# A two-layer kernel on eight cores: another order for the first eight tiles

## What is computed

```python
x = L0_attn_x
xn = layernorm(x)                                  # no scale, no shift
z, h = sigmoid(xn @ Wz.T + bz), xn @ Wh.T + bh
s = affine_scan(log(1 - z + 1e-8), z * h)          # along T
g = silu((silu(xn @ Wg.T) * (xn @ Wu.T)) @ Wd.T)   # int weights / 127
x = x + s * g
xn = layernorm(x)
q, k, v = split(xn @ W_qkv.T)
s = softmax(q @ k.T / 32) @ v
r, kk = sigmoid(mix_r(xn) @ W_r.T), mix_k(xn) @ W_k.T
g = silu(r * (relu(kk) ** 2 @ W_v.T))
x = x + s * g
```

## Time and profile before

| | us |
|---|---|
| three runs: median, lowest, highest | 1232.82, 1171.05, 1410.46 |
| the profiled execution | 1171.72 |
| its span on the slowest core (core 0) | 1170.6 |
| spans of all cores | 1168.2 to 1170.6 |
| PE busy on core 0 | 1145.4 (98%) |
| PE busy in 10 to 15, 15 to 20 and 20 to 25 us of core 0 | 3.57, 2.94, 4.13 |

### The profile page before, as it was taken

How to read it: one execution, slowest core, us unless ns; L and a number is a source line. 1 busy time by engine, 2 the same in 40 slices (tenths; PEclk the granted TensorE clock), 3 DMA queues, 4 the chain that set the end, 5 groups by cost and what they waited for, 6 DMA issues and landing times.

```text
span 1170.6 us, 15141 instructions; the slowest of 8 cores (1168.2 to 1170.6 us)
## 1 busy us (share of the span) xinstructions
PE 1145.4 (98%) x5315; PEld 527.5 (45%) x5422; DVE 550.2 (47%) x700; ACT 251.6 (21%) x317; POOL 137.6 (12%) x257
## 2 busy tenths in 40 slices
PE   5999999999999999999999999999999999999998
PEld 3444444444444444444444444444444444444444
DVE  4333331555657663225557884011134445555565
ACT  4211111122123111112212723533110110110110
POOL 3222221110111111101011122220000000000000
PEclk8999999999999999999999999999999999999999
DMA  9996678545554765545543579994000105255665
GB/s 212 211 143 103 91 121 185 108 108 103 119 103 72 168 122 81 80 81 107 107 102 61 84 127 156 150 157 112 1 19 18 37 18 121 71 124 115 138 137 160
DMA packets 96522, 126.91 MB, mean 108 GB/s; under 512 B 48192, under 2 KB 52544, under 8 KB 96448
## 3 DMA queue, kind: packets, MB, share of 16 engines
q0 software_dynamic: 31104, 65.03, 35.7%
q1 hardware_dynamic: 65344, 60.91, 19.8%
HBM read 159.47 MB, written 20.97 MB: 154 GB/s over the span
## 4 chain that ended last, share of the span: by engine, by line
PE 97%; DVE 1%; DMA 1%; issue 1%; ACT 0%; SPq 0%; POOL 0%; DVEq 0%; ACTq 0%; POOLq 0%
PE PS L156 96%; DMA S<-xtok 1%; DVE S L160 0%; PE PS L293 0%; SPq L127 0%; DVE S L284 0%; DVE S L911 0%; DVE S L306 0%; DVE BN L243 0%; ACT S L281 0%; DVE BN L244 0%; ACT S L309 0%; PE PS L880 0%; PE PS L879 0%; POOL MV L264 0%
## 5 line engine op out<-in xcount | busy, mean ns | idle before, releaser
L156 PE MATMUL PS<-S 128*128 128x512 bf16 x5157 | 1131.7, 379 | 7.4 <-ACT S L771 0.9
L156 PEld LDWEIGHTS PS<-S 128*128 128x128 bf16 x5264 | 514.6, 98 | 616.3 <-issue 4.8
L160 DVE TENSOR_TENSOR S<-S,PS 128x512 bf16<-128x512 bf16 x96 | 66.0, 688 | 182.9 <-PE PS L156 169.8
L404 ACT ACTIVATE S<-PS 128x512 bf16<-128x512 f32 x96 | 57.3, 597 | 258.5 <-PE PS L156 199.2
L851 ACT ACTIVATE S<-PS,CB 128x2048 bf16<-128x2048 f32 x16 | 31.5, 1967 | 225.0 <-DVE CB L849 209.4
L160 DVE TENSOR_TENSOR S<-S 128x512 f32<-128x512 f32 (+2 forms) x60 | 62.9, 1048 | 6.5 <-DVE S L569 0.3
L847 DVE TENSOR_REDUCE CB<-PS 128x1 f32<-128x1024 f32 x32 | 39.2, 1225 | 54.9 <-PE PS L880 33.1
L748 DVE SCALAR_TENSOR_TENSOR S<-S,PS 128x1024 f32<-128x1024 f32 x16 | 19.5, 1222 | 83.8 <-PE PS L156 83.5
L469 ACT ACTIVATE S<-PS 128x512 bf16<-128x512 f32 x32 | 19.1, 597 | 172.9 <-PE PS L156 172.9
L127 POOL DMA_DIRECT2D S<-wg x48 | 28.4, 592 | 232.6 <-PE PS L156 230.9
L798 DVE CAST S<-PS 128x512 bf16<-128x512 f32 x32 | 22.1, 692 | 48.3 <-PE PS L156 46.8
(11 more groups left out here) (77 smaller groups left out, 401.7 us busy)
## 6 DMA issues: line engine op xcount, KB each, us to landing
S<-wg POOLq DMA_DIRECT2D x48, 256.0 KB, 4.7
S<-wu POOLq DMA_DIRECT2D x48, 256.0 KB, 5.7
S<-wd POOLq DMA_DIRECT2D x16, 768.0 KB, 7.5
S<-xtok SPq DMA_DIRECT2D x16, 512.0 KB, 9.6
S<-xt SPq DMA_DIRECT2D x16, 512.0 KB, 16.2
x1s<-S SPq DMA_DIRECT2D x16, 512.0 KB, 2.6
S<-x1s SPq DMA_DIRECT2D x32, 256.0 KB, 4.4
out<-S SPq DMA_DIRECT2D x31, 256.0 KB, 3.1
```

Of the source, the lines that this page charges most:

```text
L156: ins = te.matmul(dst, l, r, start=(i == 0), stop=(i == n - 1))
L160: return DVE.did(ve.tensor_mul(o, a, b))
L404: at = ACT.did(se.activation(sil, ps(bg), AF.Silu, scale=1.0 / 127.0))
```

## The change

- Tile 1 and tile 3 are asked for by ScalarE's queue, tile 0, the identity and tile 2 by SyncE's. Tiles 4 and 5 are asked for by SyncE behind a wait for tile 1's statistics, tiles 6 and 7 and the two small matrices behind a wait for tile 3's.
- The first weight pair is asked for behind tile 1's root and bias, no longer behind tile 0's; the second pair behind tile 3's root, the third behind tile 4's, the fourth, as before, behind tile 5's.
- Tile 2's statistics and norm go to VectorE; `ln0_stats_act` is gone, and each root is for one tile. Tiles 0, 1 and 2 are copied from PSUM by ScalarE right behind their transposes, tile 3 by VectorE.
- `keep_warm` is called with 24, 8, 8 and 12 instead of 24, 4 and 10, one call behind each of the four transposes.

```diff
-        def xk_load(i):
-            xk_tok.append(dma(SYN, x_tile(i), xk[i * 128:(i + 1) * 128, :], xk_sem[i % 8]))
+        def xk_load(i, line=SYN):
+            xk_tok.append(dma(line, x_tile(i), xk[i * 128:(i + 1) * 128, :], xk_sem[i % 8]))
 
         xk_load(0)
         i_tok = dma(SYN, ident[:], identd, i_sem)
-        for i in range(1, 8):
-            xk_load(i)
-        c_tok = dma(SYN, CB[:, 0:32], cb, c_sem)
-        c_tok = dma(SYN, ones[:], onesd, c_sem)
+        xk_load(1, ACT)
+        xk_load(2)
+        xk_load(3, ACT)
...
         ln0_stats(0)
         ln0_rstd(0)
         ln0_bias(0)
-        POOL.after(xk_tok[1])
-        w_pair()
-        w_pair()
         ln0_norm(0, True)
-        ln0_transpose(0, True, False)
+        ln0_transpose(0)
         keep_warm(24)
         ln0_stats(1)
+        SYN.after(ln0_tok[1])
+        xk_load(4)
+        xk_load(5)
         ln0_rstd(1)
         ln0_bias(1)
-        ln0_stats_act(2)
+        w_pair()
         ln0_norm(1, True)
-        ln0_transpose(1, True, False)
-        keep_warm(4)
+        ln0_transpose(1)
+        keep_warm(8)
+        ln0_stats(2)
+        ln0_rstd(2)
         ln0_stats(3)
-        ln0_copy(0, True)
-        ln0_rstd(2, 2)
-        ln0_bias(2, True)
+        SYN.after(ln0_tok[3])
+        xk_load(6)
+        xk_load(7)
+        c_tok = dma(SYN, CB[:, 0:32], cb, c_sem)
+        c_tok = dma(SYN, ones[:], onesd, c_sem)
+        ln0_rstd(3)
         w_pair()
-        ln0_norm(2, True)
+        ln0_norm(2)
+        ln0_transpose(2)
+        keep_warm(8)
         ln0_norm(3)
-        ln0_transpose(3, True, False)
-        ln0_copy(1, True)
-        ln0_copy(3, True)
-        ln0_transpose(2)
-        keep_warm(10)
+        ln0_transpose(3, True)
+        keep_warm(12)
         ln0_stats(4)
         ln0_rstd(4)
         ln0_bias(4)
+        w_pair()
         ln0_norm(4, True)
         ln0_stats(5)
         ln0_rstd(5)
```

More of the change, by code:

```diff
@@ L246, in ln0_stats @@
             ln0_tok[i] = DVE.did(ve.bn_aggr(MV[:, i * 2:i * 2 + 2], b))
[L248 to L256, removed]
         def ln0_rstd(i, n=1):
@@ L266, in ln0_rstd, with ln0_bias @@
                 ln0_tok[q] = t
-        def ln0_bias(i, act=False):
-            m, f = (MV[:, 60:61], 32.0) if act else (MV[:, i * 2:i * 2 + 1], -1.0)
+        def ln0_bias(i):
             POOL.after(ln0_tok[i])
-            nb_tok[i] = POOL.did(nc.gpsimd.tensor_scalar(MV[:, 48 + i:49 + i], m, MV[:, 32 + i:33 + i], f,
-                                                         ALU.mult, ALU.mult))
+            nb_tok[i] = POOL.did(nc.gpsimd.tensor_scalar(MV[:, 48 + i:49 + i], MV[:, i * 2:i * 2 + 1],
+                                                         MV[:, 32 + i:33 + i], -1.0, ALU.mult, ALU.mult))
         def ln0_norm(i, act=False):
```

## The result

The change makes the kernel slower: 1177.41 us, median of five runs, against 1171.05; the ratio is 1.0053, with a 95% interval of 1.0041 to 1.0065. The forecast was 1170.0, and 1177.4 lies above its range of 1168.0 to 1174.0. Executions in which one die's cores ran at a lower clock, such as 1232.82 and 1410.46 us of the kernel before, are left out of every ratio and of the medians in the experiments; without them the two medians here are 1176.97 and 1170.98. The profiled execution took 1176.53 us with a span of 1175.4.

What follows compares the result with a forecast made beforehand. Bound: the start of tile 7's transpose on the slowest core, set by tiles' chain, clock and first weights' landing. About 3.3 us freed, half lost to later weights: 38.0 - 36.3 = 1.7, so 1171.7 - 1.7 = 1170.0 us, range 1168.0 to 1174.0.

Steps and rivals of the forecast that it cites:

- T7: Transpose of tile 7 on PE; its start on the slowest core sets the time, the rest being constant, 1132.6 to 1133.5 us.
- x through two queues: Start of the head: tiles 0 and 1 under way together, a loss of 1.5 us for tile 0's chain.
- s0: Start of tile 0's statistics, taken as 7.5 us instead of 5.97.
- the weights' term: First weights' landing in the head: later requests, quicker landing (8, 8.2, 8.8 and 10 us); about half of 3.3 us freed is lost.
- S = 19.8: Tiles ready for the first gate matmul at 19.8 us, about 1.6 earlier than 21.45, with full clock on the slowest core.
- The first pair: First two weights, behind tile 1's root and bias: asked for at 13.3 and 14.0 us, landing at 21.3 and 22.2.
- The second pair: Third and fourth weights, behind tile 3's root: asked for at 16.2 and 16.8 us, landing at 25.0 and 26.8.
- s3: Start of tile 3's statistics on VectorE, taken as 12.7 us, 0.9 earlier than 13.62.
- my own rule: Landing plus what remains of 14.95 us bounds T7; weights are needed at offsets 0, 1.8, 3.6 and 5.9.
- The clock as a rival by itself: Head on PE: clock falls anyway or added work runs at half clock; no gain, say 1171.5 us; chance 0.2.
- The eighth weight ... doesn't move: Tiles 8 to 15 start when the eighth weight lands; that landing was taken as unchanged.
- the slower rival: First weights land as slowly as before, 10.1 to 14.9 us; T7 2.7 us later, 1174.4 us; chance 0.2.

Runs made afterwards that it cites:

- run 2: Changed kernel with tiles 4 to 7 and the two small matrices asked for at the start, without SyncE's two waits: 1174.54 us, 1.0027.
- run 5: Compute side of the change alone: changed kernel with all x tiles in one queue at the start and weight pairs where the kernel before has them: 1171.50 us, 1.0013.
- run 12: Kernel before with tile 6's statistics, root and bias ahead of the first unit, and tiles 4 and 5 copied by VectorE: 1171.29 us, 1.0005.
- run 3: Changed kernel with tiles 1 and 3 asked for by SyncE again, so one queue for tiles 0 to 3: 1175.33 us, 1.0036.
- run 6: Transfers of the change alone: kernel before with the change's queues, its two SyncE waits and its places of the weight pairs: 1176.72 us, 1.0051.
- run 8: Compute side of the change; four tiles in one queue, tiles 4 and 5 and the first weight pair when tile 0 has landed: 1170.59 us, 1.0001.
- run 1: Changed kernel with the second weight pair right behind the first instead of behind tile 3's root: 1175.42 us, 1.0037.
- run 4: Changed kernel with the first two weight pairs behind tile 0's bias, the third behind tile 3's root, the fourth behind tile 5's: 1176.08 us, 1.0041.

## Why the prediction was wrong, step by step

- *T7 as the milestone: right, but for 0.6 us.* Span minus T7 is 1132.6 to 1134.1 in the profile after, where I had said 1132.6 to 1133.5. The up to 1.5 us over are waits for weights at 55 to 59 us on cores 1, 2, 4 and 6; in runs 2, 5 and 12 it goes up to 1136.0, so the rest is no constant.
- *x through two queues: right in kind, too small.* I took s0 = 7.5. It was 6.6 to 9.0, and 8.28 on the slowest core. Run 3 shows that it is the two queues.
- *Tile 3's statistics at 12.7:* 13.39 on the slowest core, held up by VectorE's list as assumed, from the later start.
- *"What it costs is a hole of 1 to 2 us ..., and I leave that in the weights' term": failed.* The hole was 3 us (shares of 0.54, 0.12, 0.00 and 0.36), and I then did not put it into that term: I let the weights land quicker, for fewer tiles ahead. They did so one by one (6.4 and 9.7), but the bytes that didn't move in the hole are missing for what comes behind: up to 30 us the changed kernel has moved 0.2 to 0.8 MB less than the 6.37 MB of the head.
- *Tiles' chain and clock, S = 19.8: right until the wait.* The first gate matmul came at 18.9 to 22.1, at 20.40 on core 7, with a clock of 1.00. The last 12 spare matmuls took 0.83 us, 69 ns each, on every core, as reckoned (0.064).
- *The first pair: right within 1.1 us.* Asked for at 13.80 (forecast 13.3), landed at 20.2 (21.3).
- *The second pair, "s3 + 3.5 = 16.2" and 8.8 us of landing: the step that failed.* It was asked for at 18.08 and landed at 27.76, not at 25.0. Of the 2.8 us, 0.7 is s3; 1.2 is GpSimd's own list, where tile 2's root (15.18) stands behind the first pair and tile 3's behind tile 2's, which I had called slack; 0.9 is landing. By my own rule, 27.8 + 11.35 gives T7 at 39.1, and the cores on which the clock held bear the rule out (11.5 us from the third weight to T7).
- *The clock as a rival by itself: failed.* T7 was at 42.3, 3.2 later than that, because the clock fell during the 2.93 us wait. I had priced weights and clock apart; on five of eight cores the one came with the other. I had also misread core 1, which was to speak for a clock that holds. The windows print 1.00 wherever the trace has no clock record, and core 1's first record is at 21.17 us. Ahead of it the pace was that of 1.2 GHz, as ten small matmuls in 1.27 us on core 1 before show:

```profile
19.68 1.27 PE L320 MATMUL PS<-ident 128*128 128x128 bf16 x10
```

- *"The eighth weight ... doesn't move": wrong.* It landed at 33.2 to 37.7 instead of 31.1 to 32.6, and run 2 shows what such a delay does at 57 us.
- *"Two per cent, about what a measurement of this kernel can tell from no change": wrong.* The interval of the ratio is about 0.12% wide to either side.

So the weights were late, as in the slower rival (chance 0.2, price 2.7 us), but not by its mechanism: it had each weight land as slowly as before, and they landed quicker and were asked for later, behind a hole. It cost 6 us. Runs 5 and 6 settle that it is the transfers: alone they give 1.0051, the rest alone 1.0013; run 8 takes the hole away and the loss with it. How much of the loss is the clock's stays open; runs 1 and 4 lose 0.37 and 0.41% with no fall of the clock on any core of the profiled execution.

## What to carry to other kernels

In a head that is bound by bytes, an order of transfers is judged by when the last byte that is needed has moved (here by 30 us), not by how quickly each lands: with less asked for at the start, each of the first four weights landed quicker here, and the eighth was there later. If a load is to wait so that others go first, something must already be queued that fills the engines until then. And a saving in front of a backlog is only worth what the next wait leaves of it: in runs 5 and 12 up to 2 us came back 20 us later.

## What the runs showed of the hardware

- Two tiles asked for at the same time in two queues land together, and the first one later: tiles 0 and 1 landed within 0.2 us of each other on seven of the eight cores of the changed kernel (0.7 on the eighth), tile 0 at 6.4 to 8.8 us instead of 4.7 to 6.1 with one queue (run 3).
- After waits of PE of 2.0 to 3.0 us the granted clock fell to 0.50 (1.2 GHz) on five cores of the changed kernel, for 3.4 us on four and 6.8 on core 7 (waits of 2.62, 3.03, 2.04, 2.12 and 2.93 us on cores 0, 3, 5, 6 and 7). It stayed at 1.00 on cores 1, 2 and 4 (2.88, 2.51 and 2.11), so the length of the wait alone doesn't decide it.
- The first matmuls ran near the pace of 1.2 GHz: on core 7, 24 small ones at 13.84 took 115 ns each and 12 of the same at 19.12 took 69 (127 at half clock in the earlier trace rows). The windows print 1.00 for both, but core 7's first clock record is at 16.78 us, so the 1.00 ahead of it is no reading.
